# Second layer's weights split early, parked in DRAM and brought back; routed tiles ahead of the shared experts of blocks 1 to 3

## What is computed

```python
xn = layernorm(x)
x = x + linear_attention(xn)            # 8 heads, relu(q), relu(k)
      + moe16(xn)                       # 16 experts, top 6, hidden size 176
xn = layernorm(x)
x = x + recurrence(xn) @ W_out.T + b    # s = tanh(W_in xn_t + b_in + s*gamma + beta), 512 steps in order
      + moe8(xn)                        # 8 experts, top 2, hidden 176, weights of the two made to sum to 1
      + swiglu(xn, shared weights)      # two shared experts, hidden 352
```

## Time and profile before

| | us |
|---|---|
| median of 3 runs (lowest, highest) | 717.23 (716.01, 718.45) |
| the profiled execution's own time | 718.17 |
| its span in the profile | 716.5 |
| TensorE busy | 635.1 |
| VectorE busy | 482.1 |
| ScalarE busy | 367.5 |
| GpSimd busy | 252.9 |
| mean granted TensorE clock, of full speed | 0.963 |

### The profile page before, as it was taken

The page is one execution under the profiler, slowest core; times in us unless marked ns, Lnnn a source line. Parts: engine busy times, 40 slices in busy tenths (PEclk is TensorE's granted clock), DMA queues, the critical chain, the costliest instruction groups (busy, mean ns, idle before and its releaser), DMA issues. The chain is left out here.

```text
span 716.5 us, 12798 instructions
## 1 busy us (share of the span) xinstructions
PE 635.1 (89%) x3607; PEld 345.9 (48%) x3607; DVE 482.1 (67%) x1515; ACT 367.5 (51%) x1008; POOL 252.9 (35%) x267
## 2 busy tenths in 40 slices
PE   6998999999999999899999888886867898879875
PEld 2664544544445444344444333533544576557544
DVE  7965775655526777867788865876685556676573
ACT  3444445442453555575456557455545746654540
POOL 5246222222322244321255231133411162365373
PEclk8999999999999999999999999999888999999976
DMA  8001222399999997000000000112322254573223
GB/s 309 37 1 45 89 88 89 109 359 348 349 346 349 348 346 226 0 1 1 1 30 30 0 16 29 60 37 86 87 64 60 59 150 122 136 165 119 89 75 110
DMA packets 90244, 88.94 MB, mean 124 GB/s; under 512 B 29928, under 2 KB 81224, under 8 KB 90184
## 3 DMA queue, kind: packets, MB, share of 16 engines
q1 hardware_dynamic: 84808, 73.52, 32.5%
q0 software_dynamic: 5376, 14.69, 6.7%
HBM read 22.91 MB, written 58.98 MB: 114 GB/s over the span
## 5 line engine op out<-in xcount | busy, mean ns | idle before, releaser
L1810 POOL TENSOR_TENSOR hl<-scr,hh 128x512 f16<-128x512 f32 (+2 forms) x100 | 117.1, 1171 | 324.5 <-ACT hh L1202 324.3
L1665 DVE TENSOR_TENSOR_SCAN zbuf<-gam,RING 128x32 f32<-128x32 f32 x512 | 152.5, 298 | 86.9 <-ACT RING L1232 86.1
L1232 ACT ACTIVATE RING<-zbuf 128x16 f32<-128x16 f32 x512 | 111.1, 217 | 181.7 <-DVE zbuf L1665 176.6
L673 PE MATMUL G<-xT,W 128*128 128x512 f16 (+2 forms) x600 | 148.1, 383 | 17.2 <-ACT scr L1191 14.6
L673 PE MATMUL U<-xT,W 128*128 128x512 f16 (+2 forms) x600 | 149.3, 386 | 0.0
L673 PE MATMUL Y<-hh,W 128*128 128x512 f16 x352 | 119.5, 380 | 16.3 <-POOL hl L1810 16.0
L1677 DVE TENSOR_TENSOR scr<-scr,U 128x512 f32<-128x512 f32 (+2 forms) x100 | 67.5, 675 | 54.3 <-PE U L673 41.1
L673 PEld LDWEIGHTS G<-xT,W 128*128 128x128 f16 (+3 forms) x600 | 60.2, 103 | 83.9 <-issue 22.6
L673 PEld LDWEIGHTS U<-xT,W 128*128 128x128 f16 (+3 forms) x600 | 62.5, 104 | 70.6 <-issue 3.9
L1191 ACT ACTIVATE scr<-G 128x512 f32<-128x512 f32 (+2 forms) x100 | 58.7, 587 | 66.2 <-PE G L673 65.6
L1202 ACT ACTIVATE hh<-scr 128x512 f16<-128x512 f32 (+2 forms) x100 | 61.8, 618 | 18.8 <-DVE scr L1682 11.2
(11 more groups left out here) (198 smaller groups left out, 830.5 us busy)
## 6 DMA issues: line engine op xcount, KB each, us to landing
xrows<-zeros SPq DMA_DIRECT2D x1, 22656.0 KB, 69.3
yrows<-zeros SPq DMA_DIRECT2D x1, 22656.0 KB, 138.1
stage<-weights SPq DMA_DIRECT2D x20, 384.0 KB
yrows<-scr POOLq DMA_DIRECT2D x48, 128.0 KB
stage<-weights SPq DMA_DIRECT2D x14, 256.0 KB
RING<-weights SPq DMA_DIRECT2D x8, 384.0 KB, 8.0
out<-xres SPq DMA_DIRECT2D x8, 256.0 KB, 2.5
xres<-x SPq DMA_DIRECT2D x3, 512.0 KB, 7.5
```

Source lines behind the costliest of these rows:

```text
L673: last = nc.tensor.matmul(bank_, w(wp), act(ap), start=start and n == 0, stop=stop and n == count - 1)
L1232: nc.scalar.activation(RING[:, (t + 1) % RING_T, ::2], zbuf[:, 1::2], ACT.Tanh).then_inc(state_done, 1)
L1665: nc.vector.tensor_tensor_scan(zbuf[:, :], gam[:, :], RING[:, t % RING_T, :], 0.0, ALU.mult, ALU.add)\
L1810: nc.gpsimd.tensor_tensor(hl[rows, a, :], h32[a][rows, :], hh[rows, a, :], ALU.subtract)\
```

## The change

The split of the second layer's weights moves ahead. Chunk pieces (now 28 to 41) are split in pair 10 of phase 0 and pairs 0 to 2 of phase 1, four a pair, two in each half. Their split form goes into the idle `RING`. SP copies it to a DRAM array (`park`, 128 rows of 28,160 B). The down pieces (42 to 47) follow into the ring's second half in pairs 5 to 10 of phase 1 and are parked too (88 rows of 16 KB). The first copy of inputs and VectorE's clearing of the first state now wait for the parking. In phase 3, when the dense chunks whose place it takes are done, SP brings each back into `flat` with one DMA (`bring_back`). The shared down piece is the last one (48), split in pair 4 of phase 3. The fills are issued by ScalarE, ahead of pair 5 of phase 0 and of pair 3 of phase 2. In the units, shared block 0 comes first, then all R units (3 to 26), then shared blocks 1 to 3. The shared sums use `Y[j % 2]`. Norm, routing and placing of block 3 start earlier and the norm has two parts at each step. Gathers have 16 buffers instead of 8, in the place of dense chunks 16 to 21; they stand in units 18 to 25 (two each) and 30 to 35 (3, 3, 3, 3, 3, 1), combines a unit behind in the first group. The output stores wait for each half of a block by itself.

```diff
-UNITS = ([("S", j, g) for j in (0, 1) for g in range(3)]
+UNITS = ([("S", 0, g) for g in range(3)]
          + [("R", group, q) for group in (0, 1) for q in range(TILES // 2)]
-         + [("S", j, g) for j in (2, 3) for g in range(3)])
+         + [("S", j, g) for j in (1, 2, 3) for g in range(3)])
-RING_XG, RING_YG = 4, 8
+RING_XG, RING_YG = 4, 16
...
-        LAST_PAIRS_PIECES = {4: (28,), 5: (29, 30), 6: (31, 32), 7: (33, 34), 8: (35, 36), 9: (37, 38), 10: (39, 40)}
-        UNIT_PIECES = {0: (41, 42), 1: (43,), 2: (44,), 3: (45,), 4: (46,), 5: (47,), 6: (48,)}
+        PAIR_PIECES = {(0, 10): (28, 29), (1, 0): (30, 31, 32, 33), (1, 1): (34, 35, 36, 37), (1, 2): (38, 39, 40, 41),
+                       (1, 5): (42,), (1, 6): (43,), (1, 7): (44,), (1, 8): (45,), (1, 9): (46,), (1, 10): (47,),
+                       (3, 4): (48,)}
...
+                front[5].append(("fill", (0,)))
...
+                    front[3].append(("fill", (1,)))
...
-            5: [("shared_add", (0, Y[0]))],
-            6: [("split_states", (1, 0))],
-            7: [("norm_turn", (7, Y[1])), ("rows", (3, 0)), ("split_states", (1, 1))],
-            8: [("shared_add", (1, Y[0])), ("logits", (7, Y[1][1])), ("rows", (3, 1)), ("split_states", (1, 2))],
-            9: [("inputs", (3, 0, Y[1])), ("exp", (7,)), ("split_states", (1, 3))],
-            10: [("inputs", (3, 2, Y[1]))],
-            12: [("rank", (3, Y[1][1])), ("more_inputs", (4,))],
-            13: [("scatter", (3, 0)), ("scatter", (3, 1))],
-            14: [("attend", (1, Y[1])), ("scatter", (3, 2)), ("scatter", (3, 3))],
+            5: [("shared_add", (0, Y[0])), ("norm_turn", (7, Y[1])), ("rows", (3, 0))],
+            6: [("logits", (7, Y[1][1])), ("rows", (3, 1)), ("split_states", (1, 0))],
+            7: [("inputs", (3, 0, Y[1])), ("exp", (7,)), ("split_states", (1, 1))],
+            8: [("inputs", (3, 2, Y[1])), ("split_states", (1, 2))],
+            9: [("rank", (3, Y[1][1])), ("split_states", (1, 3))],
+            10: [("scatter", (3, 0)), ("scatter", (3, 1))],
+            11: [("scatter", (3, 2)), ("scatter", (3, 3))],
+            12: [("more_inputs", (4,))],
+            14: [("attend", (1, Y[1]))],
...
-            27: [("attend", (2, Y[1]))],
+            26: [("attend", (2, Y[1]))],
+            32: [("shared_add", (1, Y[1]))],
...
-            n = ROWS // P
-            for rows, empty, done in ((xrows, zeros.bitcast(f16), filled[0]), (yrows, zeros.bitcast(f32), filled[1])):
-                sp.dma_start(rows.rearrange("(n p) d -> p n d", p=P),
-                             empty[:, :].unsqueeze(1).broadcast_to([P, n, rows.shape[1]])).then_inc(done, 16)
...
+            def park(n, pieces, view):
+                sp.wait_ge(pieces_split, pieces)
+                sp.dma_start(parked[n][0:view.shape[0], :], view).then_inc(parked_out[n], 16)
+
+            def bring_back(n, chunks, to, held):
+                sp.wait_ge(down_done, (BLOCKS - 1) * CH0 + chunks)
+                sp.wait_ge(parked_out[n], 16)
+                size = parked[n].shape[1]
+                sp.dma_start(flat[0:held, to:to + size], parked[n][0:held, :]).then_inc(parked_back[n], 16)
...
+            bring_back(0, 10, 0, P)
+            bring_back(1, 16, DOWN_AT, HF)
...
-                acc = Y[j // 2]
+                acc = Y[j % 2]
...
+                    if j < 2 and c == 0:
+                        act.wait_ge(parked_out[j], 16)
...
+            def fill(n):
+                rows, empty = ((xrows, zeros.bitcast(f16)), (yrows, zeros.bitcast(f32)))[n]
+                act.wait_ge(zeros_made, 1)
+                nc.scalar.dma_start(rows.rearrange("(n p) d -> p n d", p=P),
+                                    empty[:, :].unsqueeze(1).broadcast_to([P, ROWS // P, rows.shape[1]]))\
+                  .then_inc(filled[n], 16)
```

More of the change, by code:

```diff
@@ L431, in run_phase, with run @@
                     share[name](*args)
-                ticks, load = kinds[a]
-                def run(k, ticks=ticks, load=load, woven=woven[a]):
+                ticks, load, late = kinds[a]
+                def run(k, ticks=ticks, load=load, late=late, woven=woven[a]):
                     pieces = [load[0] * (k - load[2]) + load[1] + i for i in range(load[0])] if load else []
-                    if phase == BLOCKS - 1:
-                        pieces = LAST_PAIRS_PIECES.get(k, ()) if isinstance(k, int) else ()
-                    pair(k, tick_of(phase, k) if ticks else None, pieces, woven)
+                    pair(k, tick_of(phase, k) if ticks else None, pieces, late, woven)
                 if b - a == 1:
@@ L640, in _ @@
             load_down(DOWN_PIECE)
+            park(0, DOWN_PIECE, spare[:, 0:parked[0].shape[1]])
+            for piece in range(DOWN_PIECE + 1, SHARED_PIECE):
+                load_down(piece)
+            load_shared_down()
+            park(1, SHARED_PIECE, spare[0:HF, SPARE_DOWN_AT:2 * SPARE_DOWN_AT])
+            bring_back(0, 10, 0, P)
+            bring_back(1, 16, DOWN_AT, HF)
             for u in range(len(UNITS)):
@@ L924, in _, with pair @@
             for phase in range(BLOCKS):
-                def pair(k, tick, pieces, woven):
+                def pair(k, tick, pieces, late, woven):
                     for a in range(2):
@@ L1079, in split_sorted @@
                 elif piece < DOWN_PIECE:
-                    c = piece - CHUNK_PIECE
-                    act.wait_ge(down_done, last + 10)
-                    for src, dst in sorted_chunk(c, stage[:, a, 0:4 * P], 0):
+                    if piece == CHUNK_PIECE:
+                        act.wait_ge(pieces_split, EARLY)
+                    for src, dst in sorted_chunk(piece - CHUNK_PIECE, stage[:, a, 0:4 * P], 0):
                         ins = nc.scalar.activation(dst, src, ACT.Copy, scale=W_SCALE)
@@ L1247, in pair @@
                         step(tick, HALF * a + HALF - 1)
+                        for piece in late[a * (len(late) // 2):len(late) if a else len(late) // 2]:
+                            split_sorted(piece)
                     for a, piece in enumerate(pieces):
-                        if isinstance(piece, int) and piece >= SLOTS:
-                            split_sorted(piece)
-                        else:
-                            split_staged(piece, a)
+                        split_staged(piece, a)
                 run_phase(act, phase, pair, share, steps=True)
@@ L1281, in _ @@
                 unit_step(u, 5)
-                for piece in UNIT_PIECES.get(u, ()):
-                    split_sorted(piece)
             n = DENSE0 + len(UNITS)
@@ L1716, in pair @@
                         step_and(HALF * a + HALF - 1)
+                        for piece in late[a * (len(late) // 2):len(late) if a else len(late) // 2]:
+                            split_sorted(piece)
                     for a, piece in enumerate(pieces):
-                        if isinstance(piece, int) and piece >= SLOTS:
-                            split_sorted(piece)
-                        else:
-                            split_tail(piece, piece, stage[:, a, :])
+                        split_tail(piece, piece, stage[:, a, :])
                 run_phase(dve, phase, pair, share, steps=True)
@@ L1729, in unit_step @@
                     if u in UNIT_WOVEN:
-                        name, block_, first = UNIT_WOVEN[u]
-                        share[name](block_, first + i)
+                        name, block_, first, each = UNIT_WOVEN[u]
+                        for part in range(each):
+                            share[name](block_, first + each * i + part)
                 unit_front(u, share)
@@ L1892, in _ @@
             h_tail(DENSE0 + len(UNITS) - 1, (DENSE0 + len(UNITS) - 1) % 2)
-            for i in range(GATHERED, K1 * BATCH * BLOCKS):
-                gather(i)
 def kernel(**inputs):
```

108 lines of the change are left out of this document (57 added, 51 removed).

## The result

The changed kernel takes **714.15 us** (median of 20 runs, 710.91 to 716.47), the kernel before, beside it, 718.68 (20 runs): a ratio of **0.993**, 95% interval 0.9915 to 0.9945. It is faster, by 0.7% and not by the 2.7% forecast. The profiled execution took 714.77 with a span of 713.0 against 716.5 before.

A forecast was written before the change was run, and what follows sets the result against it. TensorE, busy 635 of 716.5 us, was taken as the bound, with idle in the last third. Gains of 33.2 us less costs of 13.5 took 718.2 to 698.5, forecast 698; range 682 to 717, likeliest 691 to 706.

The forecast's parts named there:

- 1, pieces leave phase 3: Phase 3, pairs 5 to 10: twelve chunk pieces leave, idle falls as in phase 2's like pairs, -6.2 us.
- part 2: Units 0 to 2: without pieces they and the block's turn take 13.0 us instead of 19.8, -6.8 us.
- Part 3: Block 1's shared units, moved from units 3 to 5 to 27 to 29: 3 x 4.0 instead of 20.8 us, -8.8.
- Part 4: Seven R units with block 3's work, packed into units 3 to 9: -3 us, bounds +3 and -8; other 17: 0.
- 5, units 30 to 34: S units at the end: three gathers a unit need 5.3 us on GpSimd against TensorE's 4.0, +5 us.
- Part 6: Tail from the last S unit's start: 17.7 us instead of 31.1, -13.4; bounds -8 and -15.
- Part 7: Twelve pieces in phase 1, pairs 0 to 2: +9 us, bounds +3 and +20; two in phase 0, pair 10: +0.5.
- 8, six down pieces: Phase 1, pairs 5 to 10: six down pieces at 0.5 us each, +3 us.
- 9 and 10, fill issue, parking: Fills issued by ScalarE cost 0; first parking lands near 203 us, +1, bounds 0 and +8; second parking 0.
- A: Rival: one shared descriptor generator, so ScalarE's fill holds SP's loads in phase 0, pairs 5 and 6; about 746 us, chance 0.15.
- B: Rival: contention and late parking eat the gain; 724 us at worst, 713 halfway, chance 0.14.
- C: Rival: DMA engines serve the loads first and the tail shrinks as drawn; 688 us, chance 0.19.

The follow-up runs named there:

- run 4: Changed kernel with gathers 28 to 31 issued by GpSimd after its last h_tail: 717.43 us, ratio 0.9964 to the kernel before.
- run 5: Changed kernel with VectorE's last gated product ahead of three combines, shared_add and the last two splits: 713.83 us, ratio 0.9915 to the kernel before.
- Run 6: Changed kernel with VectorE's last gated product first and GpSimd's last gathers put off: 712.39 us, ratio 0.9913 to the kernel before.
- run 3: Changed kernel's early splits, parking and fills, with unit order, fronts, banks, combines and gathers of the kernel before: 720.4 us, ratio 1.0008 to the kernel before.
- run 7: Changed kernel with block 1's splits of states moved from units 6 to 9 to units 9 to 11: 713.07 us, ratio 0.9905 to the kernel before.
- run 10: Changed kernel with splits of blocks 1 and 2 behind h's copy on ScalarE, a unit later on VectorE: 710.65 us, ratio 0.9851 to the kernel before.
- run 12: Changed kernel loading only 64 of 128 partitions of each chunk piece, so split weights are wrong: 711.34 us, ratio 0.9897 to the kernel before.

## Why the prediction was wrong, step by step

The sign, the range (682 to 717) and the removal of the wait on block 2's addition were right; the gain was 3.5 us of span where the sum said 19.7. Forecast and measured, us, from the windows of both kernels:

| part | forecast | measured |
|---|---|---|
| 1, pieces leave phase 3 | -6.2 | -6.8 |
| 2, units 0 to 2 | -6.8 | -4.0 (15.8, not 13.0) |
| 3, shared units of block 1 | -8.8 | -6.9 (13.9, not 12.0) |
| 4, seven R units; the other 17 | -3; 0 | +1.4; +0.4 |
| 5, units 30 to 34 | +5 | +2.5 (22.5) |
| 6, the tail | -13.4 | -7.4 (23.7, not 17.7) |
| 7, phase 1 to pair 4; phase 0 | +9; +0.5 | +13.7; -0.7 |
| 8, six down pieces | +3 | +3.3 |
| 9 and 10, fill issue, parking | 0; +1 | 0; 0 |
| phase 2 | 0 | +1.0 |

**Part 6 failed most (6.0).** Its term "1.0 of wait for h_tail" was 5.2: TensorE waits 0.7, 3.3 and 1.2 us for the h of three units. The last down took 2.5 where 1.3 was set and the attend 6.1 where it was 5.4, against which only what follows the attend got shorter (3.3, not 4.8). The step that failed is that the sum followed one engine only, and that one not far enough ("leaves one gather in the last unit"): the three gathers of unit 34, ahead of that unit's h, were not counted, and VectorE not at all. The profile of before has the last h like this:

```profile
694.02 0.67 DVE L1677 TENSOR_TENSOR scr<-scr,U 112x512 f32<-112x512 f32 x1
...
695.16 0.63 ACT L1202 ACTIVATE hh<-scr 112x512 f16<-112x512 f32 x1 [7.17 <-PE Y L960]
...
700.99 1.16 POOL L1810 TENSOR_TENSOR hl<-scr,hh 112x512 f16<-112x512 f32 x1
```

VectorE reaches the last gated product 8.6 us after the unit's start at 685.4. With the 0.67, 0.63 and 1.16 us of these three, the last down would start at 11.1 us even with GpSimd free; the sum had 6.2 (5.2 and 1.0). GpSimd began 5.2 us after ScalarE's h was there, so it alone stood as the releaser of the stall (3.31 us). In the changed kernel VectorE still reaches its last gated product only 9.0 us after the unit's start. Runs 4, 5 and 6 show that in the changed kernel both hold the tail. Run 6 still needs 21.2, not 17.7: 0.7, 2.2 and 0.8 us of waits for h_tail, a last down of 2.5 at a clock of 0.92 in the window, and the slower `h_tail` told of below.

**Part 4 had the wrong sign (4.4).** Its bound of +3 ("norm twice as dense") held the outcome. In the old order with the pieces gone the same seven units take 47.4 (run 3), in the new one 50.5: packing costs 3.1. "Idle here comes from ScalarE's order" was right as far as VectorE waits for ScalarE's half of a split, and runs 7 and 10 show which part of the order costs: four splits at 1.3 us each ahead of h.

**Part 7 was mis-sized (3.5 with phase 0).** The form of the sum was right: load, ScalarE, VectorE, then the buffer is free. The failing step was to keep "1.2 us of lead" from the earlier trace rows, where no fill ran, and to put the price of the fill into the rate. The lead was 4.1 us and the packets of a load took 1.1 to 1.3, so a load took 5.7 us and not 4.2, a half pair 7.58 and not 6.4; in run 12 half the bytes brought nothing. And the step asked what the change costs with the fill at pair 5, not whether it had to be there. The earlier trace rows showed that the fill ran beside phase 1 before as well, when nobody loaded.

**Parts 2 and 3 (4.7).** Unit 2 carries the copy of the sums ahead of its silu on ScalarE and their turn on TensorE, and takes 6.55 us (508.65 to 515.2); 1.0 was set for it. Part 3 took 20.8 us as its base, though the pieces leaving (part 2's kind of gain) alone bring units 3 to 5 to 16.0 (run 3): of 6.9 us the order gives only 2.1. The early half of the change came out at the forecast's nothing (-6.2 - 6.8 + 13.5 = +0.5; run 3: 1.0008), but by errors that cancel. In run 3 unit 0 starts 11.4 us later than before where the sum had 7.3, and units 0 to 2 give 5.1 and not 6.8; units 3 to 5 give 4.8 that the sum had booked to the order.

**Rivals.** A is refuted by SP's loads: no hold of tens of us. B's mechanism, contention eating the gain, is the largest single one (12 us), and 713 halfway was close to the result; but it came by way of part 7 at +14 and part 6 at -7, with parking on time and no down piece dearer. C fell: the loads are not served first. "Phase 1's first pairs near 36 us" nearly held: pairs 0 to 2 take 37.6 (153.6 to 191.2, 26.8 before). Pair 3 takes 11.6 in place of 8.7, and the +9 had nothing for it. "The last six pairs of phase 3 under 60" held (57.7).

## What to carry to other kernels

A long background transfer isn't cheap because its issue is: ask which short loads with a consumer close behind run beside it, and move it to where nobody waits for a load; here one line was worth 1.9%. A moved or packed side task costs its full length when it stands ahead of the item that the main chain waits for (h here), and nearly nothing just behind it. Where a stall's releaser is known, work out when the second-latest input would have come, before the whole stall is booked as gain.

## What was unexpected of the hardware

- **A fixed lag beside a large fill.** A 256 KB load issued while a 22.7 MB fill ran on the other queue landed 5.7 to 6.1 us after its buffer was free, one of 128 KB after 5.7, where a load of the same pieces without the fill took 2.95. All of the difference but a few tenths lies ahead of the load's first packet (3.9 to 4.5 us in place of 1.0). The Trainium skill (DMA: Bandwidth & Descriptors, Queues, rings and completion order) has each DMA engine go round the queues packet by packet; by that a small load would pay for a few packets and in proportion to its rows. The trace agrees for the packets once they move; the lag ahead of them is not of that kind.
- **VectorE and GpSimd slow each other.** The first row is from the changed kernel, the others are from the tail of run 6, in order of engine:

```profile
696.39 1.98 DVE L1610 SCALAR_TENSOR_TENSOR SH<-RING,SH 128x508 f16<-128x508 f32 x1
...
693.21 2.51 POOL L1848 TENSOR_TENSOR hl<-scr,hh 120x512 f16<-120x512 f32 x1
...
692.81 1.95 DVE L1609 SCALAR_TENSOR_TENSOR SH<-RING,SH 128x508 f16<-128x508 f32 x2
694.67 1.34 DVE L1645 SCALAR_TENSOR_TENSOR xres<-W,share_of,xres 128x256 f32<-128x256 f32 x1
```

In the changed kernel the `h_tail` of 696.38 takes 1.16 us, and the split that starts beside it 1.98 in place of 1.00: VectorE pays. In run 6 the `h_tail` of 693.21 starts while VectorE splits states and takes 2.51, in place of 1.16 for the next one; it ends 0.96 after the split does, and the combine beside it (0.48 elsewhere) takes 1.34. The Trainium skill (SBUF — State Buffer, Who interferes with whom) says that a VectorE instruction with two SBUF inputs contends with a GpSimd instruction that reads SBUF; the trace agrees. The forecast of the tail left it out: 1.0 us on the way to the last gated product in the changed kernel, 1.35 on the way to the last down in run 6.
